# A two-layer message-passing kernel: the next batch's features made ready inside the present batch, two rooms for the last radial units, and the sum over the axes on VectorE

## The reference

```python
R = jax.nn.relu(abs_distances[:, None] @ w1 + b1) @ w2 + b2
Y = spherical_harmonics(rel_vec)
Fj = features[src]
acc = acc + _NORM[i] * jnp.einsum('euv,ef,evi,ofi->euo', Rb[..., k], Yf, Fb, C)
out = out.at[dst].add(msg)
```

## Time and profile before

| what | us |
|---|---|
| median of three runs | 3802.88 |
| profiled execution | 3798.03 |
| its span, first to last instruction | 3796.3 |
| PE (TensorE) busy | 3310.6 (87%) |
| DVE (VectorE) busy | 2762.8 (73%) |
| POOL (GpSimd) busy | 2786.3 (73%) |
| ACT (ScalarE) busy | 2061.5 (54%) |

### The profile page before, as it was taken

How to read it: one execution, slowest core, us unless ns; L and a number is a source line. 1 busy time by engine, 2 the same in 40 slices (tenths; PEclk the granted TensorE clock), 3 DMA queues, 4 the chain that set the end, 5 groups by cost and what they waited for, 6 DMA issues and landing times.

```text
span 3796.3 us, 58108 instructions
## 1 busy us (share of the span) xinstructions
PE 3310.6 (87%) x17312; PEld 1902.1 (50%) x17312; DVE 2762.8 (73%) x3470; ACT 2061.5 (54%) x2391; POOL 2786.3 (73%) x2915
## 2 busy tenths in 40 slices
PE   4999999999999883399999999999999999999963
PEld 3898889898989783222323232333323232323232
DVE  5787877787878785467777777777777777777765
ACT  4777777776777660145454545454554545454520
POOL 6777777777777776677777777777777777777746
PEclk9999999999999995599999999999999999999975
DMA  4122222222122211122222222222222222222211
GB/s 100 39 57 41 52 43 43 50 44 54 40 55 43 50 48 29 39 57 53 62 55 59 55 59 55 59 58 56 62 52 62 55 59 54 59 55 59 57 28 26
DMA packets 188428, 197.65 MB, mean 52 GB/s; under 512 B 60241, under 2 KB 149427, under 8 KB 188085
## 3 DMA queue, kind: packets, MB, share of 16 engines
q1 hardware_dynamic: 95508, 149.13, 13.7%
q0 software_dynamic: 92832, 47.72, 9.7%
HBM read 134.02 MB, written 62.59 MB: 52 GB/s over the span
## 4 chain that ended last, share of the span: by engine, by line
PE 70%; ACT 12%; DVE 5%; POOL 5%; issue 5%; DMA 1%; SPq 0%; ACTq 0%; DVEq 0%; POOLq 0%
PE ps_r L940 19%; PE ps_r L990 17%; PE ps_m L1027 10%; PE ps_m L940 10%; PE ps_r L1018 8%; ACT prod_room L822 8%; POOL ngot L667 4%; DVE unit L1645 3%; PE ps_m L1037 2%; PE ps_r L1002 2%; ACT f_across L829 2%; PE ps_r L924 1%; ACT hot_s L739 1%; PE ps_m L1043 1%; ACT hot_s L742 1%
## 5 line engine op out<-in xcount | busy, mean ns | idle before, releaser
L688 POOL DMA_INDIRECT got<-x_d,idx x1564 | 1506.2, 963 | 530.6 <-issue 504.7
L822 ACT ACTIVATE prod_room<-ps_r,bias_col 128x1024 f32<-128x1024 f32 x392 | 435.9, 1112 | 780.0 <-PE ps_r L990 531.9
L940 PE MATMUL ps_r<-x_hi,hot_s 128*128 128x448 f32 x1974 | 741.6, 376 | 41.7 <-ACT hot_s L742 41.7
L1645 DVE TENSOR_TENSOR x_room<-radial_more,ps_r 128x1024 f32<-128x1024 f32 x392 | 475.0, 1212 | 384.0 <-PE ps_r L1018 252.3
L990 PE MATMUL ps_r<-hid,wc 64*128 64x512 f32 (+1 forms) x2352 | 669.8, 646 | 81.2 <-ACT prod_room L822 72.9
L940 PE MATMUL ps_r<-x_lo,hot_s 128*128 128x448 f32 x1974 | 733.0, 371 | 0.0
L739 ACT ACTIVATE hot_s<-rows,minus_row 128x512 fp32r<-128x512 f16 (+1 forms) x658 | 449.0, 764 | 244.0 <-PE ps_m L940 206.2
L1018 PE MATMUL ps_r<-ft,repeat 32*128 32x512 f32 (+1 forms) x2352 | 553.4, 639 | 1.1 <-ACT ft L848 0.6
L1645 DVE TENSOR_TENSOR unit<-prod_room,ps_r 128x1024 f32<-128x1024 f32 x392 | 451.1, 1213 | 106.9 <-PE ps_r L1018 102.0
L940 PEld LDWEIGHTS ps_r<-x_hi,hot_s 128*128 128x128 f32 x1974 | 378.3, 192 | 75.5 <-issue 43.0
L990 PEld LDWEIGHTS ps_r<-hid,wc 64*128 64x128 f32 x2352 | 178.8, 186 | 448.8 <-ACT prod_room L822 255.3
(11 more groups left out here) (203 smaller groups left out, 4438.4 us busy)
## 6 DMA issues: line engine op xcount, KB each, us to landing
hid<-weight_t SPq DMA_DIRECT2D x196, 256.0 KB
run_d<-runs_t SPq DMA_DIRECT2D x194, 256.0 KB
got<-x_d,idx POOLq DMA_INDIRECT x1564
rows<-code_d SPq DMA_DIRECT2D x47, 160.0 KB
frame_d<-x_sb SPq DMA_DIRECT2D x7, 1008.0 KB, 4.5
frame<-frame_d SPq DMA_DIRECT2D x98, 72.0 KB
frame_b<-frame_d SPq DMA_DIRECT2D x98, 72.0 KB
rows<-code_d SPq DMA_DIRECT2D x47, 128.0 KB
```

What stands on the lines that cost most here:

```text
L688: pool.indirect_dma_start(got[k][:, t, :], None, x1_d, bass.IndirectOffsetOnAxis(ap=idx[k][:, t:t + 1], axis=0)).then_inc(got2_landed[k], 16)
L822: act.activation(radial_s[u][:, :, 0:w], radial_slot[:, :, 0:w], ACT.Identity, bias=bias_col[:, c:c + 1]).then_inc(radial_copied, 1)
L940: mm = pe.matmul(found[BANK_OF[k][g]], hot_s[k][:, a, g, :], part[:, a * LN * D:(a + 1) * LN * D], start=(a == 0 and n == 0), stop=(a == B ...
L1645: dve.tensor_tensor(product[q][h][:, :, 0:w], radial_s[u][:, :, 0:w], spread_slot[(k + s_ + 1) % 2][:, :, 0:w], ALU.mult).then_inc(multipl ...
```

## The change

- The rotation, the scalars' copy, the feature turn and the copy into `ft` for batch b+1 move into batch b: on VectorE between m5 and m6, on ScalarE behind the copy of radial unit 4 (scalars and indices) and behind that of unit 5 (the turned features), on TensorE behind r5. `ft` gets a second buffer. The turned features go to the bank that the messages use, and no longer to a spread slot; the slots no longer alternate with the parity of the batch.
- The radial units 4 and 5 get two rooms each in SBUF, one for each parity, so that their copies wait for products two batches back and not one.
- The sum over the axes leaves TensorE. VectorE adds the three products by two additions and writes the messages into SBUF, where the scan reads them; `add_axes` and its semaphore go.
- The orders of the three engines are written anew. TensorE: s0, sum 3 (batch before), s1, turning of the messages (batch before), s2, r0, r1, sum 0, s3, sum 1, r2, s4, s5, sum 2, r3, r4, r5, feature turn of the next. VectorE: m0, m1, turn back with the two additions, m2, m3, m4, scan, m5, rotation of the next, m6, m7. ScalarE: copy of the sums, masks, copies of units 0 to 2, runs, ReLU, copies of units 3 and 4, scalars, indices, copy of unit 5, `ft`.

```diff
-        ft = sb("ft", [P, QUAD * P])
+        ft = [sb(f"ft{k}", [P, QUAD * P]) for k in range(2)]
+        radial_extra = sb("radial_extra", [P, 2 * QUAD * P])
...
-        radial_more = sb("radial_more", [P, 2, 2 * QUAD * P])
+        radial_more = sb("radial_more", [P, 3, 2 * QUAD * P])
-        scalars_s = f_across[1][:, :, :, :, :].rearrange("p t a b v -> p (t a b v)")[:, 0:T * MUL].rearrange("p (t u) -> p t u", u=MUL)
+        terms2 = f_across[1][:, :, :, :, :].rearrange("p t a b v -> p (t a b v)").rearrange("p (o t) -> p o t", t=T)
...
+
+        def radial_at(u, k):
+            return radial_s[u if u < 4 else 4 + 2 * k + u - 4]
+
-        terms2 = ps_m[:, 0, :].rearrange("p (o t) -> p o t", t=T)
+        turned_p = ps_m[:, 0, :]
...
@@ -813,13 +818,15 @@
                 act.activation(hid[k][:, :], hid[k][:, :], ACT.Relu, bias=b1_col[:, :],
                                scale=w1_col[:, :]).then_inc(hid_ready, 1)
 
-            def copy_radial(b, u, w=QUAD * P):
+            def copy_radial(b, k, u, w=QUAD * P):
 
                 c, h = RADIAL_UNITS[u]
                 act.wait_ge(radial_ready, UNITS * b + u + 1)
-                if not isinstance(b, int) or b > 0:
-                    act.wait_ge(multiplied, len(PRODUCTS) * (b - 1) + (1, 2, 3, 4, 7, 8)[u])
-                act.activation(radial_s[u][:, :, 0:w], radial_slot[:, :, 0:w], ACT.Identity,
+                if u < 4 and (not isinstance(b, int) or b > 0):
+                    act.wait_ge(multiplied, len(PRODUCTS) * (b - 1) + u + 1)
+                if u >= 4 and (not isinstance(b, int) or b > 1):
+                    act.wait_ge(multiplied, len(PRODUCTS) * (b - 2) + u + 3)
+                act.activation(radial_at(u, k)[:, :, 0:w], radial_slot[:, :, 0:w], ACT.Identity,
                                bias=bias_col[:, c:c + 1]).then_inc(radial_copied, 1)
 
             def copy_summed(b, w=QUAD * P):
...
@@ -828,43 +835,54 @@
                     act.wait_ge(messages_ready, b)
                 act.copy(summed_t[:, 0:w], summed_p[:, 0:w]).then_inc(summed_copied, 1)
 
+            def copy_scalars(b, k, rounds, n):
+
+                act.wait_ge(got2_landed[k], 16 * (T * rounds + n))
+                if not isinstance(b, int) or b > 1:
+                    act.wait_ge(turned, b - 1)
+                act.copy(turned_in[k][:, 0:n, 0:MUL], got[k][:, 0:n, 0:MUL]).then_inc(f0_copied, 1)
+
+            def copy_turned(b, k, w=QUAD * P):
+
+                act.wait_ge(turned, b + 1)
+                if not isinstance(b, int) or b > 1:
+                    act.wait_ge(spread_ready, UNITS * (b - 1))
+                act.copy(ft[k][:, 0:w], turned_p[:, 0:w]).then_inc(ft_ready, 1)
+
             def layer1(i, last=False):
                 for k in range(2):
                     b = 2 * i + k
                     first, final = isinstance(b, int) and b == 0, last and k == 1
-                    n = TL if final else T
-                    w = TL // QUAD * P if final else QUAD * P
+                    n = TL if last else T
+                    w = n // QUAD * P
                     if not first:
                         copy_summed(b - 1)
-                    act.wait_ge(got2_landed[k], 16 * (T * i + n))
-                    if not isinstance(b, int) or b > 1:
-                        act.wait_ge(turned, b - 1)
-                    act.copy(turned_in[k][:, 0:n, 0:MUL], got[k][:, 0:n, 0:MUL]).then_inc(f0_copied, 1)
-                    copy_radial(b, UNITS - 1, w)
-                    act.copy(idx[k][:, :], src_all[:, bass.ds((b + 2) * T, T)]).then_inc(idx_ready, 1)
-                    act.wait_ge(turned, b + 1)
-                    if not first:
-                        act.wait_ge(spread_ready, UNITS * b)
-                    act.copy(ft[:, 0:w], spread_slot[k][:, 0, 0:w]).then_inc(ft_ready, 1)
-                    if not first:
                         masks2(b - 1, 1 - k)
                     if not final:
-                        later = TL // QUAD * P if last else QUAD * P
-                        for u in range(4):
-                            copy_radial(b + 1, u, later)
+                        for u in range(3):
+                            copy_radial(b + 1, 1 - k, u, w)
                     if not first:
                         carry_and_turn(b - 1, 1 - k)
                     if not last:
                         relu(k, i + 2)
                     if not final:
-                        copy_radial(b + 1, 4, later)
+                        copy_radial(b + 1, 1 - k, 3, w)
+                        copy_radial(b + 1, 1 - k, 4, w)
+                        copy_scalars(b + 1, 1 - k, i + k, n)
+                        if not last:
+                            act.copy(idx[1 - k][:, :], src_all[:, bass.ds((b + 3) * T, T)]).then_inc(idx_ready, 1)
+                        copy_radial(b + 1, 1 - k, 5, w)
+                        copy_turned(b + 1, 1 - k, w)
 
             act.wait_ge(loaded_net, 96)
             relu(0, 1)
             relu(1, 1)
             act.wait_ge(bias_ready, 1)
-            for u in range(UNITS - 1):
-                copy_radial(0, u)
+            for u in range(UNITS):
+                copy_radial(0, 0, u)
+            copy_scalars(0, 0, 0, T)
+            act.copy(idx[0][:, :], src_all[:, 2 * T:3 * T]).then_inc(idx_ready, 1)
+            copy_turned(0, 0)
             layer1(0)
             layer1(1)
             with act.Fori(2, PAIRS - 1) as i:
...
@@ -996,26 +1014,26 @@
 
                 pe.wait_ge(rotated_in, b + 1)
                 pe.wait_ge(f0_copied, b + 1)
-                if not isinstance(b, int) or b > 0:
-                    pe.wait_ge(multiplied, len(PRODUCTS) * b - 1)
+                if not isinstance(b, int) or b > 1:
+                    pe.wait_ge(back_ready, b - 1)
                 for j in range(w // P):
-                    mm = pe.transpose(spread_slot[k][:, 0, j * P:(j + 1) * P],
+                    mm = pe.transpose(turned_p[:, j * P:(j + 1) * P],
                                       turned_in[k][:, QUAD * j:QUAD * (j + 1), :].rearrange("p t f -> p (t f)"), ident[:, :])
                 mm.then_inc(turned, 1)
 
             def spread_features(b, k, s, w=QUAD * P):
 
                 c, h = SPREADS[s]
-                slot = spread_slot[(k + s + 1) % 2]
+                slot = spread_slot[s % 2]
                 if s == 0:
                     pe.wait_ge(ft_ready, b + 1)
-                    if not isinstance(b, int) or b > 0:
-                        pe.wait_ge(multiplied, len(PRODUCTS) * b)
+                if s < 2 and (not isinstance(b, int) or b > 0):
+                    pe.wait_ge(multiplied, len(PRODUCTS) * (b - 1) + s + 7)
                 if s > 1:
                     pe.wait_ge(multiplied, len(PRODUCTS) * b + (2, 4, 5, 6)[s - 2])
                 for t in range(2):
                     group = slice((2 * h + t) * D, (2 * h + t + 1) * D)
-                    mm = pe.matmul(slot[:, t, 0:w], repeat[group, c, :], ft[group, 0:w], start=True, stop=True)
+                    mm = pe.matmul(slot[:, t, 0:w], repeat[group, c, :], ft[k][group, 0:w], start=True, stop=True)
                 mm.then_inc(spread_ready, 1)
 
             def sum_products(b, q, w=QUAD * P):
...
@@ -1031,19 +1049,10 @@
             def turn_messages(b, w=QUAD * P):
 
                 pe.wait_ge(summed_copied, b + 1)
-                if not isinstance(b, int) or b > 0:
-                    pe.wait_ge(scanned, BATCHES + b)
+                pe.wait_ge(ft_ready, b + 1)
                 for j in range(w // P):
                     mm = pe.transpose(ps_m[:, 0, j * P:(j + 1) * P], summed_t[:, j * P:(j + 1) * P], ident[:, :])
                 mm.then_inc(messages_ready, 1)
-
-            def add_axes(b, n=T):
...
@@ -1052,33 +1061,29 @@
                     short = TL // QUAD * P
                     w = short if final else QUAD * P
                     later = short if last else QUAD * P
+                    spread_features(b, k, 0, w)
                     if not first:
                         sum_products(b - 1, 3)
+                    spread_features(b, k, 1, w)
+                    if not first:
                         turn_messages(b - 1)
-                    turn_features(b, k, w)
+                    spread_features(b, k, 2, w)
                     if not final:
                         radial(b + 1, 1 - k, 0, later)
-                    spread_features(b, k, 0, w)
-                    spread_features(b, k, 1, w)
-                    if not first:
-                        add_axes(b - 1)
-                    if not final:
                         radial(b + 1, 1 - k, 1, later)
-                    spread_features(b, k, 2, w)
                     sum_products(b, 0, w)
+                    spread_features(b, k, 3, w)
                     sum_products(b, 1, w)
                     if not final:
                         radial(b + 1, 1 - k, 2, later)
-                    spread_features(b, k, 3, w)
-                    if not final:
```

(54 more changed lines are left out.)

39 lines of the change are left out of this document (6 added, 33 removed).

## The result

The changed kernel takes 4449.06 us (median of 4, 4427.11 to 4499.3) against 3800.95 (4 runs, 3797.0 to 3805.24): a ratio of 1.1686, 95% interval 1.164 to 1.1731. The prediction, 4150 with a range up to 4315, had the direction, but saw only about half of the loss of 648. A batch now takes 20.88 + (4449.3 - 3796.3) / 97 = 27.6 us.

What follows compares the result with a forecast made beforehand. TensorE's in-order list bound the kernel, with GpSimd's gathers close (20.7 us a batch). 17.7 us work plus 5.3 pauses, taken as 22.9, plus 1.6 for the clock gave 24.5 against 20.88, times 97: about 4150 us, range 3975 to 4315.

Steps and rivals of the forecast that it cites:

- the price of the clock: TensorE in layer 1: a clock fall costs up to 3.3 us, one every second batch, 1.6 us a batch.
- The earlier trace: Profile before, start of layer 1: after a 1.9 us pause the clock stayed at 0.50 for 6.8 us of nearly constant work.
- The other that I called the same, in layer 0: Profile before, 304.6 to 311.2 us: claimed to show the clock at 0.50 with TensorE nearly always busy.
- The end of the range: Upper end, with one clock fall of 3.3 us in each batch: 26.2 us a batch, 4315 us.
- The pauses: TensorE's idle in the new batch: 5.3 us, 4.1 between adjacent radial units and 1.2 before the first spread.
- the rival with the clock at 1.00: Pauses cost time but the clock stays up: 22.9 us a batch, about 4000 us; chance 0.28.
- the bunch r3 to r5: Last three radial units, back to back on TensorE: bare pauses of 1.36 us each, little work, so the clock may fall.
- the pause between r0 and r1: First two radial units, now adjacent on TensorE: the second waits a bare 1.36 us for the first one's eviction.
- The rules weighed there: Skill page on TensorE's clock: only long idle gaps harm, or frequent small pauses suffice; the second was weighed heavier.
- my bound of 0.7: VectorE's second new addition, writing with a stride: between 0.3 and 0.7 us, taken as 0.56.
- loses nothing below 22.9: GpSimd's gathers wait for indices at about 22 us, then need 20.7 for 16: no loss below a 22.9 us batch.
- My rival "GpSimd binds": Removed matmuls count and pauses are hidden, so gathers set a batch of 20.7 us or less: 3785 us; chance 0.06.

Runs made afterwards that it cites:

- fillers: The changed kernel with four idle-time matmuls a batch, results never read, in TensorE's pauses: 3983.57 us, ratio 1.0476.
- before_bunched: The kernel before with only radial units 3, 4 and 5 side by side behind sum 2, copies of 3 and 4 behind the runs and ReLU: 4408.75 us, 1.1594.
- tail_fillers: The changed kernel with only two idle-time matmuls a batch, between radial units 3 and 4 and between 4 and 5: 4046.43 us, 1.0637.
- axes_alone: The kernel before with only the sum over the axes moved from four TensorE matmuls to two VectorE additions, scan terms in SBUF: 4093.96 us, 1.0764.
- units_spaced: The changed kernel with only TensorE's order rewritten, the radial units spread apart again: 3815.76 us, 1.0042.
- psum_terms: The kernel of spaced_filled with the terms of the scan back in PSUM and one more copy for the scalars: 3792.71 us, 0.9983.
- spaced_filled: The kernel of units_spaced with two idle-time matmuls a batch, between radial units 1 and 2 and before unit 4: 3826.27 us, 1.0065.
- relu_late: The kernel of both_orders with ScalarE's ReLU moved to the end of the batch: 4258.04 us, 1.1197.
- both_orders: The changed kernel with TensorE's and ScalarE's orders rewritten, radial units spread over the batch, ReLU early on ScalarE: 4378.76 us, 1.1506.

## Why the prediction was wrong

*The step that failed* is the price of the clock: "What follows s0 is nearly 5 us without a pause, so the clock comes back. A fall costs half of such a stretch, up to 3.3 us", and one of them in every second batch, 1.6 us. Measured, the clock cost 465 / 97 = 4.8 us a batch, more than the upper bound I gave. Both terms were too small: the falls came once a batch, not in every second one, and lasted 12.9 us in the mean, not 6.8. The stretch behind s0 brought it back in none of the rows shown: in the short fall the clock was back before s0, in the long one 11 us without a pause did not bring it back. The earlier trace rows had a stretch at 0.50 with 6.09 of 6.80 us busy, and I read it as the length of a fall; it was only one case, in which the clock did return. The other that I called the same, in layer 0, was not: TensorE was busy for 4.05 of its 6.60 us. Why one fall ends after 3.5 us and the next lasts over 20 is open. The end of the range, 26.2 us a batch, rested on the same 3.3, and the batch took 27.6.

*The pauses* were right: 22.9 us a batch at full clock against 22.71 in fillers, 4.1 us of bare evictions against 3.9, 1.2 before s0 against 0.9 (1.27 where the clock is up). The 183 us measured stand against 97 x 2.02 = 196. So the rival with the clock at 1.00, 4000 us, is what fillers ran (3984). The second rooms and the early features were not tried alone; the agreement of 22.71 with 22.9 leaves them little.

*Which step brings the clock down:* I saw the bunch r3 to r5, and before_bunched and tail_fillers bear that out. I did not see that `add_axes` covered the copy of r0. The prediction says that without it, and nothing else moved, a batch would fall to 18.5 us and GpSimd would bind; axes_alone is that case, with the two additions on VectorE, and its batch takes 23.98. In the changed order I did charge the pause between r0 and r1, 1.36 us against 1.30 measured, but no fall of the clock for it. The two do not add: 607 and 292 alone, 648 for the whole change. In the kernel after, sum 3, the messages and other pieces stand elsewhere, so the axes' share there is not told apart.

*The rules weighed there:* by the Trainium skill (TensorE: Matmul & The Clock Gate, HAM oscillation), which holds only long idle gaps to be harmful, the clock would have stayed up. Measured, it does not: pauses of 1.29 us twice, or of 1.98 once, were followed by 0.50. Its section A second HAM failure mode: psum-queue depth-cycling, by which small pauses that come often are enough, agrees: with the pauses filled the clock went from 0.76 to 1.00. Here it matters how they lie: in units_spaced, with one pause of 1.29 us a batch and shorter ones, the clock was at 0.96.

*VectorE:* the first addition took 0.546 as priced (0.56), the second 0.817, outside my bound of 0.7. The stride alone is not the cause, since in psum_terms, where it writes to PSUM, it took 0.57. The excess is at most 0.26 us a batch.

*GpSimd* "loses nothing below 22.9": right for this kernel, where it waits 457.4 us for indices. What was missing is that the additions and the scan in SBUF lengthen its gathers, from 964 ns to 995, and 1000 in spaced_filled, and so raise its floor from the 20.7 us of the prediction to 21.1, above the batch of the kernel before. So the change, with the terms of the scan in SBUF, gained in no order of TensorE that I tried: units_spaced and spaced_filled end at that floor. My rival "GpSimd binds", at 3785, is near what psum_terms runs (3793), with the order of spaced_filled and the terms back in PSUM.

## What to carry to other kernels

Before taking a matmul out of an in-order list, look at which eviction it covers: removed work that hid a copy leaves a pause, and a pause can cost more through the clock than through its own length: in the kernel after 465 us against 183. Price a fall by how long the clock stays down in the rows, and test it with idle-time matmuls in the pauses: four a batch took 465 us off. And when one engine issues without waiting for anyone, as GpSimd here, look at what its neighbour's operands do to each issue before reordering a third engine.

## What the runs showed of the hardware

- The granted clock fell in the last unit after two pauses of 1.29 us with 1.13 us of work between, and stayed at 0.50 through 10.97 us of work in 11.00. With a single pause of 1.29 in a batch and shorter ones (units_spaced) it was at 0.96 in the mean; after a single one of 1.98 (relu_late), 2.62 (axes_alone) or 3.47 (both_orders) it fell.
- More work made the kernel shorter: with four matmuls more in each batch it took 3984 us at a clock of 1.00 (fillers), without them 4449 at 0.76.
- A gather of 0.94 us took 1.49 beside a scan with both inputs in SBUF, and 0.94 beside the same scan with its terms in PSUM. The addition that reads and writes SBUF lay beside one of 1.24; with its result in PSUM and its inputs still in SBUF, one beside it took 1.11. The additions were not tried alone.
